# Selective scans of the first image: state drives moved from GpSimd to TensorE, C weighting from VectorE to GpSimd

## The reference

```python
x_dbl = einsum('bkdl,kcd->bkcl', xs, x_proj_weight)   # dt rank rows, 16 rows of B, 16 rows of C
dt = softplus(dt_proj(x_dbl) + bias)                  # (channel, position)
h = 0
for l in range(L):                                    # for every channel and each of 16 states
    h = exp(dt[l] * A[n]) * h + (dt[l] * u[l]) * B[n, l]
    y[l] += h * C[n, l]
y = y + D * u
```

## Time and profile before

| what | us |
|---|---|
| median of three runs | 5670.18 (5666.58 to 5673.89) |
| span of the profiled execution | 5675.5 |
| VectorE busy | 4557.4 (80%) |
| GpSimd busy | 4089.3 (72%) |
| TensorE busy | 4823.6 (85%) |
| ScalarE busy | 3512.8 (62%) |

### The profile page before, as it was taken

One profiled execution on the slowest core, in us unless ns is written; L12 is line 12 of the kernel. 1 busy time (PEld: TensorE's weight loads), 2 busy tenths in 40 slices (PEclk: granted clock), 3 DMA queues, 4 the chain that ended last, 5 costly groups with the idle time before them and its releaser, 6 DMA issues. The chain is left out here.

```text
span 5675.5 us, 64660 instructions
## 1 busy us (share of the span) xinstructions
PE 4823.6 (85%) x19381; PEld 3055.2 (54%) x19381; DVE 4557.4 (80%) x4619; ACT 3512.8 (62%) x5364; POOL 4089.3 (72%) x3128
## 2 busy tenths in 40 slices
PE   6787796778989887888999988888988988888998
PEld 2232242236666645555666645555666654556777
DVE  6999947977999957996999966996999985896544
ACT  4444353337877857766887866775878765775222
POOL 6999917957999935985999953995999962984111
PEclk8898898898999999998999999998999999999999
DMA  5666405426787715645777833654778752562110
GB/s 206 230 219 229 155 21 190 156 97 244 264 280 270 267 58 179 226 164 189 273 280 262 280 119 134 217 199 151 270 267 281 259 194 79 199 225 94 42 49 28
DMA packets 341663, 1070.72 MB, mean 189 GB/s; under 512 B 31546, under 2 KB 119462, under 8 KB 334776
## 3 DMA queue, kind: packets, MB, share of 16 engines
q1 hardware_dynamic: 341304, 1066.50, 53.8%
HBM read 1052.69 MB, written 13.68 MB: 188 GB/s over the span
## 5 line engine op out<-in xcount | busy, mean ns | idle before, releaser
L1009 PE MATMUL banks<-ident,prod 128*128 128x128 f32 x4752 | 766.9, 288 | 390.4 <-DVE prod L1310 288.1
L1009 PEld LDWEIGHTS banks<-ident,prod 128*128 128x128 f32 x4752 | 561.1, 145 | 793.4 <-DVE prod L1310 549.6
L1301 DVE TENSOR_TENSOR_SCAN banks<-banks,h 128x512 f32<-128x512 f32 x594 | 723.4, 1218 | 87.3 <-ACT banks L1149 49.2
L455 PE MATMUL banks<-prod,ident 128*128 128x512 f32 x972 | 556.6, 715 | 275.9 <-DVE prod L630 212.0
L1252 POOL TENSOR_TENSOR h<-lane,Bb 128x512 f32<-128x512 f32 x576 | 723.6, 1274 | 57.1 <-DMA Bb<-half_rows 36.1
L1149 ACT ACTIVATE banks<-lane,A 128x512 f32<-128x512 f32 x864 | 581.5, 687 | 249.8 <-DVE prod L1310 82.3
L537 ACT ACTIVATE banks<-delta_first,A 128x1024 f32<-128x1024 f32 x288 | 321.2, 1117 | 517.4 <-DVE prod L630 434.1
L1081 PE MATMUL banks<-w_a,Cb 128*128 128x384 f32 x1536 | 552.6, 488 | 0.0
L455 PEld LDWEIGHTS banks<-prod,ident 128*128 128x128 f32 x972 | 198.3, 220 | 622.2 <-DVE prod L630 360.4
L1301 DVE TENSOR_TENSOR_SCAN banks<-banks,half_carry_a,h 128x512 f32<-128x512 f32 x396 | 505.8, 1277 | 9.2 <-ACT banks L1149 5.2
L1252 POOL TENSOR_TENSOR h<-half_du_a,Bb 128x512 f32<-128x512 f32 x384 | 483.1, 1276 | 15.2 <-DMA Bb<-half_rows 11.8
(11 more groups left out here) (441 smaller groups left out, 11436.1 us busy)
## 6 DMA issues: line engine op xcount, KB each, us to landing
Bb<-half_rows SPq DMA_DIRECT2D x576, 512.0 KB, 4.3
Cb<-half_rows SPq DMA_DIRECT2D x288, 512.0 KB, 4.4
w_a<-w_in SPq DMA_DIRECT2D x256, 576.0 KB, 6.1
Bb<-rows SPq DMA_DIRECT2D x144, 512.0 KB, 4.2
Cb<-rows SPq DMA_DIRECT2D x144, 512.0 KB, 3.8
w_b<-w_in SPq DMA_DIRECT2D x128, 576.0 KB, 6.1
half_C_a<-half_rows SPq DMA_DIRECT2D x128, 512.0 KB, 6.8
C_first<-rows SPq DMA_DIRECT2D x40, 1024.0 KB, 7.8
```

The source lines that it names most:

```text
L455: mm = eng.matmul(ps[:, c, :], m.ident[:, :], src[:, cols(c)], start=n == 0, stop=added(s) == (i + 1) * N, skip_group_check=True)
L1009: mm = eng.matmul(ps[:, 0, at], src[:, at], m.ident[:, :], start=n == 0 and k == 0, stop=added(s) == (i + 1) * N, is_transpose=True, skip_ ...
L1301: eng.tensor_tensor_scan(flip(to), flip(slot(s)), flip(m.dBu[:, s % DRIVES, :]), initial, ALU.mult, ALU.add).then_inc(st.scanned, 1)
```

## The change

The diff replaces the order of `lane_scans` by another:

- For 12 of 16 states (all but `n` = 0, 4, 8, 12; in the first lane of a call only the odd ones) the drive comes from TensorE. `du` is turned by eight 128 x 128 transposes (`turn_du`) and kept in SBUF by a ScalarE copy (`keep_du`). B's rows are turned once per direction (`turn_b`, `keep_b`), and ScalarE builds from them 12 x 8 diagonal matrices of 128 x 128 (`build`, 4 in each of 24 steps around a change of direction). `drive` on TensorE is then eight products of a turned block of `du` with a diagonal, into the PSUM slot. For those states ScalarE writes the decays into an SBUF ring of two, and VectorE's scan reads one operand from each.
- GpSimd weighs 12 states (`n % 4 != 3`), VectorE four. `held` has three buffers, `prod` one.
- `add` is now eight transposes of 128 x 128, so the sum is accumulated turned; at the end of a lane ScalarE copies it out (`copy_sum`), TensorE turns it back (`back`), and `take` reads it from banks 6 and 7.
- C's rows come through a ring of four for every lane; B's rows only for the states that GpSimd drives.
- The norm lanes are other lanes (3, 5, 6, 9, 10, 11), projections come one lane earlier. Unused arguments of `layer_norm` go.

```diff
-    SLOTS, DRIVES, PRODS, HELD, BRING = 2, 2, 2, 2, 4
-    PAIRS = N // 2
+    TILES = len(lanes) // len(directions)
+    SLOTS, RING, CRING, BRING, HELD = 2, 2, 4, 2, 3
     WORK = 6
-    PROJECT_AT, LOW_AT, STORE_AT, DT_AT = (0, 2), (4, 6), 7, 7
-    MAGNITUDE_AT, EXP_AT, LOG_AT, DELTA_AT, DU_AT = 10, 11, 12, 12, 14
-    TAKE_AT, BEHIND = 1, 2
-    C_AT = {STORE_AT: (0,), 8: (1,), 9: (2,), 11: (3,), 13: (4,), 15: (5,)}
-    C_LATE = {1: (6,), 3: (7,)}
-    CENTRE_AT, CENTRED_AT, SQUARE_AT, VARIANCE_AT, RSTD_AT, NORM_AT, STORE_NORM_AT = (0, 1, 3), (4, 4, 6), (6, 7, 7), 6, 9, 10, 12
+    COPY_AT = 2
+    BACK_AT, TAKE_AT, DT_AT, MAGNITUDE_AT, LOG_AT, DELTA_AT, DU_AT = 4, 5, 6, 8, 9, 9, 10
+    PROJECT_AT, LOW_AT, STORE_AT = 10, (12, 13), 12
+    TURN_DU_AT = 15
+    NORM_LATER = 4
+    CENTRE_AT, CENTRED_AT, SQUARE_AT, VARIANCE_AT, RSTD_AT, NORM_AT, STORE_NORM_AT = (2, 2, 4), (4, 4, 5), (5, 6, 6), 6, 7, 8, 10
...
+    BY_POOL_DRIVE, FIRST_LANE_DRIVE = (0, 4, 8, 12), tuple(range(0, N, 2))
+    STATES = [n for n in range(N) if n not in BY_POOL_DRIVE]
+
+    def by_tensor(s):
+
+        return s % N not in (BY_POOL_DRIVE if s >= N else FIRST_LANE_DRIVE)
 
     def by_pool(s):
-        return s % N % 3 == 1
-
-    LANE_POOL = sum(by_pool(n) for n in range(N))
+
+        return s % N % 4 != 3
...
+    builds_at, built, before_first = {}, {}, []
+    halves = 0
+    for d in range(len(directions)):
+        order = [n for n in STATES if d or n not in FIRST_LANE_DRIVE] + [n for n in STATES if not d and n in FIRST_LANE_DRIVE]
+        begin = d * TILES * N - N + 2 if d else -2
+        for k, n in enumerate(order):
+            for half in range(2):
+                at = begin + 2 * k + half
+                (builds_at.setdefault(at, []) if at >= 0 else before_first).append((d, n, half))
+                halves += 1
+            built[d, n] = halves
...
+    def vacated(eng, s):
+
+        if s >= SLOTS:
+            old = s - SLOTS
+            if by_pool(old):
+                eng.wait_ge(st.scanned, old + 1)
+            else:
+                eng.wait_ge(st.prod, own(old) + 1)
...
+            def load_c(s):
+                d = lanes[s // N].direction
+                if s >= CRING:
+                    old = s - CRING
+                    if by_pool(old):
+                        eng.wait_ge(st.pooled, pooled(old) + 1)
+                    else:
+                        eng.wait_ge(st.prod, own(old) + 1)
+                eng.wait_ge(st.stored, 16 * (d + 1))
+                eng.dma_start(m.C[:, s % CRING, :], rows[d % 2, N + s % N:N + s % N + 1, :].to_broadcast([P, L])).then_inc(
+                    st.c[s % CRING], 16)
...
+            def turn_b(d):
+
+                if d:
+                    eng.wait_ge(st.du_kept, d * TILES)
+                eng.wait_ge(st.low, (d + 1) * NH)
+                for k in range(TT):
+                    mm = eng.matmul(ps[:, WORK + 1 if d else 0, k * N:(k + 1) * N], low[0:N, block_of(k)], m.ident[0:N, 0:N],
+                                    start=k == 0, stop=True, skip_group_check=True)
+                mm.then_inc(st.b_turned, 1)
...
+            def turn_du(i):
+
+                eng.wait_ge(st.du, i + 1)
+                if i and projects(i - 1):
+                    eng.wait_ge(st.low, (lanes[i - 1].direction + 2) * NH)
+                for k in range(TT):
+                    mm = eng.matmul(in_bank(WORK, k), m.du[:, i % 2, block_of(k)], m.ident[:, :], start=k % (HALF // P) == 0,
+                                    stop=True, is_transpose=True, skip_group_check=True)
+                mm.then_inc(st.du_turned, 1)
+
+            def drive(s):
+
+                i, n = s // N, s % N
+                eng.wait_ge(st.du_kept, i + 1)
+                eng.wait_ge(st.diagonal, built[lanes[i].direction, n])
+                vacated(eng, s)
+                for k in range(TT):
+                    mm = eng.matmul(in_bank(2 + 2 * (s % SLOTS), k), m.du_turned[i % 2][:, block_of(k)],
+                                    diagonal(n)[:, block_of(k)], start=k % (HALF // P) == 0, stop=True, skip_group_check=True)
+                mm.then_inc(st.driven, 1)
...
-                for c in range(NH):
-                    mm = eng.matmul(ps[:, c, :], m.ident[:, :], src[:, cols(c)], start=n == 0,
-                                    stop=added(s) == (i + 1) * N, skip_group_check=True)
+                if s == first_add[i]:
+                    if i:
+                        eng.wait_ge(st.copied, i)
+                    else:
+                        eng.wait_ge(st.b_kept, 1)
+                for k in range(TT):
+                    mm = eng.matmul(in_bank(0, k), src[:, block_of(k)], m.ident[:, :],
+                                    start=s == first_add[i] and k % (HALF // P) == 0, stop=place[s] == all_added[i],
+                                    is_transpose=True, skip_group_check=True)
                 mm.then_inc(st.summed, 1)
+
+            def back(i):
+
+                eng.wait_ge(st.copied, i + 1)
+                if i + 1 < len(lanes):
+                    eng.wait_ge(st.du_kept, i + 2)
+                if i + 2 < len(lanes) and fresh(i + 2):
+                    eng.wait_ge(st.b_kept, lanes[i + 2].direction + 1)
+                if i + 1 in norm_of:
+                    eng.wait_ge(norms.st.logged, norm_of[i + 1] + 1)
+                for k in range(TT):
+                    mm = eng.matmul(in_bank(WORK, k), m.du[:, i % 2, block_of(k)], m.ident[:, :], start=k % (HALF // P) == 0,
+                                    stop=True, is_transpose=True, skip_group_check=True)
+                mm.then_inc(st.back, 1)
...
+            turn_b(0)
             dt_product(0)
-            for s in range(STEPS):
+            turn_du(0)
+            for s in range(STEPS + 2):
                 i, n = s // N, s % N
+                if s + 1 < STEPS and by_tensor(s + 1):
+                    drive(s + 1)
+                if s >= 2 and by_pool(s - 2):
+                    add(s - 2)
+                if s >= STEPS:
+                    continue
                 if not by_pool(s):
                     add(s)
-                if n >= BEHIND and by_pool(s - BEHIND):
-                    add(s - BEHIND)
-                if fresh(i + 1) and n in PROJECT_AT:
-                    project(i + 1, PROJECT_AT.index(n))
+                if n == 0 and i + 1 < len(lanes) and fresh(i + 1):
+                    turn_b(lanes[i + 1].direction)
                 if i in norm_of and n in CENTRE_AT:
-                    centre(i, CENTRE_AT.index(n))
+                    for k in range(CT):
+                        if n == CENTRE_AT[k]:
+                            centre(i, k)
                 if i in norm_of and n == VARIANCE_AT:
                     variance(i)
-                if n == DT_AT + (i in norm_of) and i + 1 < len(lanes):
+                if i and n == BACK_AT + later(i):
+                    back(i - 1)
+                if i + 1 < len(lanes) and n == DT_AT + later(i):
                     dt_product(i + 1)
+                if projects(i) and n == PROJECT_AT:
+                    for c in range(NH):
+                        project(i + 2, c)
+                if i + 1 < len(lanes) and n == TURN_DU_AT:
+                    turn_du(i + 1)
+            back(len(lanes) - 1)
...
+            def build(d, n, half):
+
+                if half == 0 and d:
+                    eng.wait_ge(st.driven, tensor_before[(d * TILES - 1) * N + n + 1])
+                eng.wait_ge(st.b_kept, d + 1)
+                for k in range(half * TT // 2, (half + 1) * TT // 2):
+                    ins = eng.activation(diagonal(n)[:, block_of(k)], m.ident[:, :], ACT.Copy, scale=scales(d, k, n))
+                ins.then_inc(st.diagonal, 1)
+
+            def keep_du(i):
+
+                eng.wait_ge(st.du_turned, i + 1)
+                if i >= 2:
+                    eng.wait_ge(st.driven, tensor_before[(i - 1) * N])
+                eng.activation(m.du_turned[i % 2], flat(WORK), ACT.Copy).then_inc(st.du_kept, 1)
...
+                to = ring[s % RING]
+                if by_tensor(s):
+                    if s >= RING:
+                        eng.wait_ge(st.scanned, s - RING + 1)
+                else:
+                    to = slot(s)
+                    vacated(eng, s)
                 a = lanes[i].a_at + n * CT
-                eng.activation(slot(s), m.delta[:, i % 2, :], ACT.Exp,
-                               scale=lanes[i].A[:, a:a + 1]).then_inc(st.decay, 1)
+                eng.activation(to, m.delta[:, i % 2, :], ACT.Exp, scale=lanes[i].A[:, a:a + 1]).then_inc(st.decay, 1)
+
+            def copy_sum(i):
+
+                eng.wait_ge(st.summed, all_added[i])
+                eng.wait_ge(st.dbu, led((i + 1) * N))
+                eng.wait_ge(st.du_turned, i + 1)
+                eng.activation(m.du[:, i % 2, :], flat(0), ACT.Copy).then_inc(st.copied, 1)
...
+                if n == 0:
+                    keep_du(i)
```

(40 more changed lines are left out.)

259 lines of the change are left out of this document (105 added, 154 removed).

## The result

The changed kernel takes 5704.34 us (median of four runs, 5695.72 to 5710.76) against 5669.41 for the kernel before beside it: 1.006 times, 95% interval 1.0047 to 1.0072. Forecast was 5655, so the sign is wrong; the time is inside the range. Repeated later on, it took 5707.12 (1.0066, 1.0054 to 1.0078).

A forecast was written before the change was run, and what follows sets the result against it. VectorE and GpSimd, full and balanced, were taken to bound the kernel. Plain lanes -56, norm lanes -7, builds +10 and ends +7 gave -46; clock falls +31 made -15, so 5655 us, range 5600 to 5725.

The forecast's parts named there:

- Balance before, VectorE's and GpSimd's floors: Both engines full before, at 102.97 and 102.10 of 108.2 us; after, 42.9 and 40 us a lane, neither holding it.
- The schedule at full clock: Plain lanes: waits for TensorE's drives give groups of 13.6, 12.25, 12.15, 11.4, so 49.4 us against 54.1; twelve lanes, -56.
- TensorE's clock: Idle stretches ahead of own adds: one clock fall of three a lane, at 1.7 us, in 18 lanes: +31.
- rival 2: Clock falls in every long idle stretch, three a plain lane: +51, 5720 us; decides from 1.5 falls a lane; chance 0.18.
- the row of 2.91: Earlier profile's idle stretch of 2.91 us, after which four TensorE records took 3.30 instead of 1.98; 2.04 us brought no fall.
- The sign named for rival 2: In the changed profile, a mean granted TensorE clock below 0.85 would show that rival 2 holds.
- C ring: C's rows, asked for at latest 1.1 us into a group, land about 4 us later, used 9 or more after: no cost.
- the sign named for it: C loads ending VectorE's or GpSimd's idle time in the changed profile would show the ring's lead was wrong.
- Norm lanes: Six lanes with centre, variance and normalize: 57.2 us against 58.3 before, together -7.
- Builds on ScalarE: Four builds a step take 1.3 us, mostly hidden; 3.5 us for each of three changes of direction, +10.
- Ends: Stage start about 3 us (turn_b, turn, copy, first drive at half clock), stage end 0.6; two stages, +7.
- rival 5: Transposes don't hold TensorE's clock up, so each of four groups starts slow: 5830 us; chance 0.02.

The follow-up runs named there:

- the zero products: Changed kernel plus two 512-column products by a zero tile on TensorE ahead of own adds 3 (not in norm lanes), 11 and 15: 5670.06 us, 0.9999.
- the row of C in time: Changed kernel with the norm tile's store and next tile's load issued two steps later (STORE_NORM_AT 12 instead of 10): 5681.72 us, 1.0023.
- late adds: Changed kernel with own adds of states 3, 7 and 11 three steps later and that of 15 one step later: 5628.95 us, 0.9926.

## Why the prediction was wrong

- *Balance before, VectorE's and GpSimd's floors*: right. Both engines wait after the change.
- *The schedule at full clock*: right to 1%. A plain lane without a fall is 49.8 to 49.9 us (with the zero products) where 49.4 was forecast; by groups 13.8, 12.3, 12.6, 11.0 against 13.6, 12.25, 12.15, 11.4. The prices of transposes and drives held, and scan 0 to scan 1 is 5.4, of which 3.1 idle (3 forecast).
- *TensorE's clock*: **the step that failed.** "One fall of the three, at 1.7 us", 18 falls and +31. There were 27, that is 1.5 a lane, at about 50/27 = 1.85 us: +50, of which 8 to 12 came only with the late rows of C. The number of falls was mis-sized more than their price. A fall at a head costs up to 2.6 where turn and drive 1 are both slowed, as above, and 3.3 in one lane behind a late row; elsewhere 1.4 to 1.7. "It decides from 1.5 falls a lane on" was the point given for rival 2, and that is where the kernel landed. The idle stretches before own adds are 2.35 and 3.00 us (2.6 and 3.4 forecast), on both sides of the row of 2.91 that I set as the border, and both kinds fell. The sign named for rival 2, a mean granted clock below 0.85, was no good: the clock was 0.92 in both stages and the falls came all the same. And counting idle stretches alone can't give the number: some falls came behind none (185.5 us, above).
- *C ring*: **the second step that failed**, as the sign named for it says (waits for rows of C). "A request can stand behind one that waits for GpSimd; the same 4 us cover it": I looked at the waits in SP's order and not at the 1.5 MB that the change had moved ahead of a row. 6.8 us of waiting in five norm lanes, 15 to 19 with the falls behind it (25 between the medians).
- *Norm lanes*: 57.2 forecast, 58.9 without falls: 45.3 for the first twelve states against 45.0, and 13.6 for the last group against 12.25, of which the row of C is 1.35. Left are 0.4 a lane, 2 to 3 in all.
- *Projections*: missed. `project` stands behind step 10 in lanes 1, 4 and 7, and drive 13 waits for it; below, TensorE from the last product of L422 on, then VectorE's scan 13. Step 12 to 13 is 4.9 us, not 2.6: 3 x 2.3 = +7.

```profile
143.59 0.59 PE L422 MATMUL banks<-big,w0x 128*44 128x512 f32 x1
144.11 1.96 PE L484 MATMUL banks<-ident,prod 128*128 128x128 f32 x16
145.91 1.95 PE L466 MATMUL banks<-diagonals_first,Cb 128*128 128x128 f32 x16
```

```profile
147.96 2.29 DVE L729 TENSOR_TENSOR_SCAN prod<-h,banks 128x1024 f32<-128x1024 f32 x1 [2.58 <-PE banks L466]
```

- *Builds on ScalarE*: four builds take 1.27 us (1.3 forecast) and are hidden. The cost of a change of direction is `turn_b`, 2.0 x 3 = 6 of the 10 forecast: size near, place wrong.
- *Ends*: about right. 5.7 us more lie between the stages. The first scan starts 4.9 us later (50.77 against 45.86), but only 1.4 of that is the change's: `turn_b` puts 2.0 us between the last projection and `dt_product`, where 0.7 were. The projections ahead of it took 8.1 instead of 5.3 us, and 5.3 again in the repeat, and all started 0.8 later; kernels with the old scans in layer 0 started at 48.59 and 50.02 in their traces. So +7 against +7, and the other 3.5 are chance.
- *Transposes and the clock* (rival 5): wrong in its size, 5830 with a slow start of each group. The fast head above starts on sixteen transposes at full clock, and plain lanes without a fall are mostly transposes and drives. The rule of the Trainium skill (TensorE: Matmul & The Clock Gate, Part 4), that the full clock does not engage in transposes, does not hold in these traces: eight of them take 1.04 us at full clock and 1.91 at half. But that they count for less than drives is not refuted: the falls behind no idle stretch all came behind transposes and a narrow product, and the earlier trace rows has a stretch that mixes transposes with other products. That part stays open.

In sum, for the lanes of the profiled executions: -22 was forecast from first to last scans (-56, -7, +10, +31), +16.9 came. The difference of 39 is, by estimates from the traces, clock +19, the row of C +7, norm lanes +3, projections +7, plain lanes +5, directions -4, and +2 in the first lanes. With the ends it is +27.5 by the end of layer 1's stage. The rest of the program, which is unchanged, was 9 us shorter in that execution (it varies by some 14 us over these profiles), which is chance, and with the profiled execution being the fastest of its four it is why the two spans differ by 18.4 and the medians by 35. That 5704 lies inside the range doesn't make the account right: the forecast's own case was a gain of 15.

No single miss made the sign. With 18 falls at 1.7 the kernel would be at about 5704 - 19 = 5685, and with the row of C in time it ran at 5681.72, both still above 5669. The late row and half of the cost of the falls act on one place, the head of a lane; putting the turn first there (5648.64) turned the sign by itself.

## What to carry to other kernels

Before work is moved to an engine with room, list what stands ahead of it in that engine's order, in every kind of lane: a turn behind an add that waits for VectorE cost 2.3 us a lane here, and putting it first made the changed kernel 1.0% faster. The same holds for a DMA queue, and there the bytes ahead of a request count, not only the waits. When TensorE's work moves onto the path, its clock falls move onto it too: price each by the chain of work behind it, and take their number from a trace of a kernel with such stretches rather than from a border between two rows. Falls came here behind idle stretches down to 2.2 us (late adds: a drive at 196.64 us took 3.65 us behind 2.21 us of idle time) and behind none.
